# Hybrid block on one core: one ring of normalised rows, features read in place, and a wait ahead of GpSimd's additions

## The chip, the cores and the metric

The kernel runs on one core of one Trainium2 chip. The metric is the device time of one execution, in microseconds (us), as the median of several runs. The core has five engines with instruction streams of their own: TensorE (PE, with its weight loads shown as PEld), VectorE (DVE), ScalarE (ACT), GpSimd (POOL) and SyncE (SP), which here only issues transfers. They meet through semaphores. All share the on-chip memory SBUF; matmul results land in the eight banks of PSUM.

## What is computed

The input `x` is 4 sequences of 1024 rows of 256 numbers, f32, so 4096 rows. Four layers follow one another, each on the layer-normalised rows and added back to `x`:

```python
x = x + recurrent(_layernorm(x))   # LRU: a complex linear recurrence along time
x = x + sparse(_layernorm(x))      # same weights both times
x = x + attention(_layernorm(x))   # 8 heads of 64, keys and values through a rank-64 latent
x = x + sparse(_layernorm(x))
```

The recurrent layer, per chunk of time:

```python
u = einsum('btd,edh->ebth', x, W_in) + b_in          # three products: real, imaginary, o
h = scan(h = lam * h + gamma * (u[0] + i u[1]))       # lam = exp(-nu + i theta)
out = h.real @ W_mid[0] - h.imag @ W_mid[1] + o
y = gelu(out @ w1 + b1) @ w2 + b2 + out
y = layernorm(y) * ln_g + ln_b
```

The sparse layer, with two score branches ("out" and "in") that share one form:

```python
xc = einsum('ngf,gf->ng', x.reshape(n, 64, 4), conv_w) + conv_b
xa = gelu(batchnorm(xc))                               # statistics over all 4096 rows
score = softmax(xa @ lin_w.T + lin_b)                  # 256 scores of a row
out_branch = top32(score_out) * (x @ weight)           # the other 224 columns are zero
in_branch  = (top32(score_in) * x) @ weight
return out_branch + in_branch + bias
```

## The kernel before

`x` stays in SBUF from the first layer to the last, as 32 tiles of 128 rows. Each engine has its own block of code that runs the layers one after the other; all order is made by semaphores, and the order on each engine is written out by hand.

**Recurrent layer** (about 33 to 288 us of the span). It goes over 8 chunks of 512 rows with `over_chunks`, which calls each engine's `lru_step(n, c, behind, ahead1, ahead2, ahead4)`. The steps are pipelined: in step n VectorE makes `sums` (L1235, L1236), two `scan` pairs (L1244) and `turned_back` (L1252, L1253, L1258, L1261) of chunk n+1, the statistics and `centred` of chunk n-1, `turned_in` (L1227, products of PSUM and a table in SBUF) of chunk n+2, and layer-norm statistics of chunk n+4 (`ln_stats`, only while n+4 < 8) and of the finished chunk n-1 (`next_stats`). VectorE counts its ten main steps of a chunk on `l_dve`. TensorE in step n makes the o-product and the state product of chunk n (L1584, L1597), the input products of chunk n+2 (`lru_u`, L1556, in two halves), and the two products of the gated part (L1612, L1624 to L1630). GpSimd makes in step n, in this order: `turned_back` part 0 of chunk n+1 (L545), `rstd2(n-1)` (L557, L559), `turned_back` part 1 (L545), `residual(n-1)` (L565: x + y, 128x1024), `rstd(n+4)` (L532 to L538), `add_ln_bias(n+2)` (L550: x + ln_b, 128x1024) and `next_rstd(n-1)` (L577 to L585). Before step 0 it makes `add_ln_bias(0)`, `turned_back(0, 0)`, `rstd(2, 2)`, `turned_back(0, 1)`, `add_ln_bias(1)`.

**Sparse layers** (288 to 500 us and 1208 to 1418 us), `ffn(f)` on each engine, f = 0 and 1. ScalarE first applies the gelu to the features `xcT` (128 x 4096): the first two tiles of 128 columns into two small buffers `xa` (L972), then all eight chunks of 512 columns in place (L977), chunk 0 last because the small buffers are read from it. Then 32 tiles of 128 rows run in a software pipeline. For tile t ScalarE makes a normalised copy of the rows for the transposes (`ffn_z`, into `zf`, L878), the transposed copy (`ffn_zT`, L894), a copy of the tile's features (`ffn_xa`, L929), the logits' copy (`ffn_logits`, L900), the exponentials (`ffn_exp`, L913), exponentials with the winners masked (`ffn_rest`, L920), `ffn_sT`, `ffn_fs`, `ffn_gs` (L947, L942, L935), and a second copy of the same normalised rows for the gating (`ffn_zs`, into `zs`, L878 too, since both call `z_tile`). VectorE finds the 32 largest of 256 scores twice per tile: 8 MAX8 (L1380) and 8 MATCH_REPLACE8 (L1385), and one reciprocal (L1406). GpSimd's `tail` (L663 to L682) makes 7 elementwise operations; L667 multiplies the weights by `zs`. TensorE makes the transposes (L1694, L1720) and products (L1701, L1703, L1711, L1724). In the first sparse layer each engine also calls `head(t)`, which prepares the attention of sequence 0: ScalarE normalises 8 tiles (L1012) in tiles 8 to 15 and copies transposes (L1020), keys and queries in tiles 12 to 28.

**Attention** (500 to 1194 us) is not touched.

## Time and profile before

| | |
|---|---|
| median of 3 runs | 1422.08 us (1419.39 to 1425.52) |
| the profiled execution | 1419.8 us |
| its span, first to last instruction | 1418.1 us |
| PE busy | 1219.2 us (86%) |
| DVE busy | 1183.4 us (83%) |
| ACT busy | 1094.3 us (77%) |
| POOL busy | 992.4 us (70%) |

In the rows further down, a timeline line gives start and duration in us, engine, line, operation, what it writes and reads, and its count; neighbouring instructions of one line are merged into one row (x2, x4), and a bracket gives the engine's idle time before it and what ended that. A stretch (two times joined by a colon) gives its length and the busy time of each engine within it. Buffers carved out of the large scratch tile all show as `arena`, PSUM as `banks`.

The chain of work that ended last is PE 43%, DVE 22%, issue 17%, ACT 13%, POOL 4%. These shares are averages over layers with different limits, so the busy time of each engine is read stage by stage. The page's slices for the whole run (each digit is the busy share of one fortieth of the span, in tenths; PEclk is the granted TensorE clock):

```profile
PE   4999989757677679999999999999999999667776
DVE  7999999489999988777787778877878854799997
ACT  3332333688899679999999998999998994898886
PEclk9999999989999999999999999999999999799997
```

### The profile page before, as it was taken

What the parts mean: (1) busy time and instruction counts of PE and PEld (TensorE: products, weight loads), DVE (VectorE), ACT (ScalarE), POOL (GpSimd) and SP (SyncE); (2) the same over time, 40 slices, a digit from 0 to 9 for tenths busy, and PEclk for the clock granted to TensorE, in tenths of its full rate; (3) what the DMA queues carried; (4) which work ended last, traced back from release to release, by engine and by line L of the source; (5) the groups of instructions that cost most, each with busy time, mean ns of one, the idle gap of its engine ahead of it and who ended that gap; (6) DMA issues with size and microseconds to landing.
All of it is one profiled execution on the core that took longest, in us unless ns stands there. A gap on an engine that the chain in (4) does not pass through costs nothing.

```text
span 1418.1 us, 30913 instructions
## 1 busy us (share of the span) xinstructions
PE 1219.2 (86%) x10172; PEld 746.1 (53%) x10172; DVE 1183.4 (83%) x3173; ACT 1094.3 (77%) x2471; POOL 992.4 (70%) x1129
## 2 busy tenths in 40 slices
PE   4999989757677679999999999999999999667776
PEld 2455445434444335565666666666666667344443
DVE  7999999489999988777787778877878854799997
ACT  3332333688899679999999998999998994898886
POOL 4356753368788867767877677787777874398887
PEclk9999999989999999999999999999999999799997
DMA  6200000000000000000000000000000000000000
GB/s 169 74 1 1 0 0 1 1 1 1 1 1 1 1 1 2 2 3 2 2 2 2 2 2 2 2 2 2 2 2 2 2 2 1 1 31 16 31 16 31
DMA packets 27067, 14.84 MB, mean 10 GB/s; under 512 B 15062, under 2 KB 26652, under 8 KB 26908
## 3 DMA queue, kind: packets, MB, share of 16 engines
q1 hardware_dynamic: 26908, 12.87, 3.5%
q8 instruction: 82, 1.34, 0.4%
q14 instruction: 77, 0.63, 0.1%
HBM read 8.60 MB, written 4.19 MB: 9 GB/s over the span
## 4 chain that ended last, share of the span: by engine, by line
PE 43%; DVE 22%; issue 17%; ACT 13%; POOL 4%; DVEq 0%; DMA 0%; SPq 0%; POOLq 0%; ACTq 0%
PE banks L1848 6%; PE banks L1850 5%; DVE arena L1385 5%; PE banks L1837 5%; DVE arena L1380 4%; ACT arena L1056 4%; PE banks L1798 4%; PE banks L1774 3%; PE banks L1866 3%; PE banks L1865 3%; PE banks L1867 3%; ACT arena L1064 2%; DVE arena L1244 2%; DVE arena L1227 2%; POOL arena L726 2%
## 5 line engine op out<-in xcount | busy, mean ns | idle before, releaser
L726 POOL TENSOR_TENSOR arena<-arena 128x512 f16<-128x512 f32 x384 | 440.6, 1164 | 156.9 <-ACT arena L1064 152.1
L1056 ACT ACTIVATE arena<-banks 128x512 f32<-128x512 f32 x512 | 304.3, 600 | 53.8 <-PE banks L1850 49.9
L1459 DVE TENSOR_REDUCE arena<-banks 128x1 f32<-128x512 f32 x512 | 327.2, 679 | 9.5 <-PE banks L1837 6.4
L1064 ACT ACTIVATE arena<-arena 128x512 f16<-128x512 f32 x512 | 316.3, 633 | 0.0
L1865 PE MATMUL banks<-arena 128*128 128x65 f16 x2048 | 214.4, 193 | 6.1 <-POOL arena L726 5.8
L1866 PE MATMUL banks<-arena 128*128 128x64 f16 x2048 | 214.5, 195 | 0.0
L1867 PE MATMUL banks<-arena 128*128 128x65 f16 x2048 | 213.6, 192 | 0.0
L1483 DVE TENSOR_TENSOR arena<-arena 128x512 f16<-128x512 f32 x128 | 106.3, 830 | 125.0 <-ACT arena L1064 124.6
L1865 PEld LDWEIGHTS banks<-arena 128*128 128x128 f16 x2048 | 190.9, 96 | 35.3 <-issue 9.3
L1385 DVE MATCH_REPLACE8 arena<-arena 128x256 f32<-128x256 f32 x512 | 205.8, 409 | 1.1 <-issue 0.8
L1848 PE MATMUL banks<-arena 128*128 128x512 f16 x512 | 194.1, 379 | 14.2 <-ACT arena L1056 12.3
L1866 PEld LDWEIGHTS banks<-arena 128*128 128x128 f16 x2048 | 190.3, 97 | 28.3
L1380 DVE MAX8 arena<-arena 128x8 f32<-128x256 f32 x512 | 190.2, 413 | 13.6 <-ACT arena L900 9.3
L1837 PE MATMUL banks<-arena 128*128 128x512 f16 x512 | 194.3, 381 | 4.2 <-DVE arena L1459 4.2
L1850 PE MATMUL banks<-arena 128*128 128x512 f16 x512 | 193.7, 378 | 0.0
L1867 PEld LDWEIGHTS banks<-arena 128*128 128x128 f16 x2048 | 190.4, 99 | 0.0
L1724 PE MATMUL banks<-fW,arena 128*128 128x256 f32 x256 | 81.8, 447 | 42.8 <-ACT arena L947 42.8
L1837 PEld LDWEIGHTS banks<-arena 128*128 128x128 f16 x512 | 57.9, 113 | 71.5 <-DVE arena L1459 11.9
L1848 PEld LDWEIGHTS banks<-arena 128*128 128x128 f16 x512 | 50.4, 98 | 57.9 <-ACT arena L1056 35.8
L1724 PEld LDWEIGHTS banks<-fW,arena 128*128 128x128 f32 x256 | 47.5, 206 | 63.1 <-ACT arena L947 58.6
L1711 PE MATMUL banks<-fW,arena 128*128 128x256 f32 x256 | 78.7, 438 | 0.0
L781 ACT ACTIVATE zT<-banks 128x512 f32<-128x512 f32 x48 | 26.4, 601 | 64.6 <-PE banks L1543 64.6
(200 smaller groups left out, 2681.8 us busy)
## 6 DMA issues: line engine op xcount, KB each, us to landing
x<-in_L_attn_a_x SPq DMA_DIRECT2D x8, 512.0 KB, 3.9
out<-x SPq DMA_DIRECT2D x8, 512.0 KB, 2.9
arena<-arena SPq DMA_DIRECT2D x64, 1.0 KB, 1.9
arena<-in_L_attn_a_W_in SPq DMA_DIRECT2D x1, 768.0 KB, 5.7
arena<-in_L_attn_a_W_mid SPq DMA_DIRECT2D x1, 512.0 KB, 7.4
arena<-in_L_attn_a_w_w SPq DMA_DIRECT2D x2, 256.0 KB, 7.7
arena<-in_L_attn_b_Wq SPq DMA_DIRECT2D x1, 512.0 KB
arena<-in_L_attn_b_Wo SPq DMA_DIRECT2D x1, 512.0 KB
```

The source lines that it names most:

```text
L726: nc.gpsimd.tensor_tensor(pr_lo[c][:, kt, :], pr[:, kt, :], pr_hi[c][:, kt, :], ALU.subtract).then_inc(a_lP, 1)
L1056: nc.scalar.activation(pr[:, kt, :], ps[6 + kt % 2][:, :], ACT.Exp, scale=SM_SCALE).then_inc(a_P, 1)
L1064: nc.scalar.activation(pr_hi[c][:, kt, :], pr[:, kt, :], ACT.Copy).then_inc(a_hi, 1)
L1380: nc.vector.max(m8[p][:, i, r, :], src).then_inc(f_k[i], 1)
L1385: nc.vector.match_replace(wk[p][:, i, r % 2, :], m8[p][:, i, r, :], src, TAKEN).then_inc(f_k[i], 1)
L1459: nc.vector.tensor_reduce(mx_half[c][:, i // 2, i % 2:i % 2 + 1], ps[n % MAX_BANKS][:, :], X, ALU.max).then_inc(a_mx, 1)
L1837: mm(ps[n % MAX_BANKS][:, :], every[:, j, :], kA[B % 2][:, half * CH:half * CH + CH], start=True, stop=True).then_inc(a_mps, 1)
L1848: mm(o[:, :], kA[B % 2][:, kt * P:kt * P + P], qA[:, slot, c * CH:c * CH + CH], start=True, stop=False)
L1850: mm(o[:, :], kB[B % 2][:, kt * P:kt * P + P], qB[:, slot, c * CH:c * CH + CH], start=False, stop=True).then_inc(a_sps, 1)
L1865: mm(o, pr_hi[c][:, kt, js], lat[B % 2][:, kt, 0:1 + HD], start=kt == 0, stop=False)
L1866: mm(o[:, 1:1 + HD], pr_hi[c][:, kt, js], lat[B % 2][:, kt, 1 + HD:], start=False, stop=False)
L1867: last = mm(o, pr_lo[c][:, kt, js], lat[B % 2][:, kt, 0:1 + HD], start=False, stop=kt == KT - 1)
```

## The change

1. Sparse layers: `zs` and `ffn_zs` are gone. `zf` becomes a ring of four buffers (`Z_RING = 4`), written once per tile by `ffn_z`; both the transposes and GpSimd's product (L667) read it. `ffn_z` waits until the product of the tile four before has been made.
2. Sparse layers: `xa`, `ffn_xa` and the copies of features (L929) are gone; TensorE's logits read `xcT` in place. The gelu runs in place over tile 0, tile 1, the other half of chunk 0, then chunks 1 to 7.
3. Recurrent layer: a new GpSimd wait, `turned_whole(n)`, holds until all ten VectorE steps of chunk n are done. It stands ahead of `residual(n-1)` in each step that has a next chunk, and ahead of `add_ln_bias(0)`. `add_ln_bias(0)` moves behind both parts of `turned_back(0)` and `rstd(2, 2)`; `add_ln_bias(1)` moves into step 0.

```diff
--- before.py
+++ after.py
@@ -38,6 +38,7 @@
 GROUP = 4
 GROUPS = NH // 2
 Q_RING = 4
+Z_RING = 4
 
 
 B_IN, P_LOG, B_MID, W1B, W2B = 0, 6, 12, 16, 18
@@ -158,10 +159,8 @@
         after_rows = room[0]
 
 
-        zf = [carve([D]) for _ in range(2)]
-        zs = [carve([D]) for _ in range(2)]
+        zf = [carve([D]) for _ in range(Z_RING)]
         zfT = [carve([KB2, P]) for _ in range(2)]
-        xa = [carve([P]) for _ in range(2)]
         lg = [carve([2, D]) for _ in range(2)]
         wk = [carve([2, 2, D]) for _ in range(2)]
         m8 = [carve([2, ROUNDS, 8]) for _ in range(2)]
@@ -281,8 +280,7 @@
         f_bn = sem("f_bn_step")
         f_xa_all = sem("f_gelu")
         f_z = sem("f_z")
-        f_zs = sem("f_z_gating")
-        f_xa = sem("f_xa")
+        f_g01 = sem("f_gelu_first_tiles")
         f_tps = sem("f_zT_psum")
         f_zT = sem("f_zT")
         f_lps = sem("f_logits_psum")
@@ -544,6 +542,10 @@
                 pool.wait_ge(l_dve, n * L_STEPS + 4)
                 nc.gpsimd.tensor_tensor((pa, pb)[part], g[0], (cosT, sinT)[part], ALU.mult).then_inc(l_pool, 1)
 
+            def turned_whole(n):
+
+                pool.wait_ge(l_dve, n * L_STEPS + L_STEPS)
+
             def add_ln_bias(n):
                 pool.wait_ge(s_z, n + 1)
                 rows = x[:, bass.ds(n * TPC, TPC), :]
@@ -604,11 +606,11 @@
                     nc.gpsimd.affine_select(out=cvs[:, k, i, :], in_=cvb[:, i, k * P:k * P + P],
                                             compare_op=ALU.is_equal, fill=0.0, base=0,
                                             pattern=[[1, P]], channel_multiplier=-1).then_inc(s_prep, 1)
+            turned_back(0, 0)
+            turned_back(0, 1)
+            rstd(2, 2)
+            turned_whole(0)
             add_ln_bias(0)
-            turned_back(0, 0)
-            rstd(2, 2)
-            turned_back(0, 1)
-            add_ln_bias(1)
 
             def lru_step(n, c, behind, ahead1, ahead2, ahead4):
                 if ahead1:
@@ -617,9 +619,11 @@
                     rstd2(n - 1)
                 if ahead1:
                     turned_back(n + 1, 1)
+                    turned_whole(n + 1)
                 if behind:
                     residual(n - 1)
                 if n == 0:
+                    add_ln_bias(1)
                     rstd(3, 3)
                 if ahead4:
                     rstd(n + 4, n + 4)
@@ -663,8 +667,8 @@
                 nc.gpsimd.tensor_tensor(dd[p][:, 1, :], ex[p][:, 1, :], exr[p][:, 1, :],
                                         ALU.subtract).then_inc(f_d, 1)
                 pool.wait_ge(f_d, T * 2 + 1)
-                pool.wait_ge(f_zs, T + 1)
-                nc.gpsimd.tensor_tensor(sx[p], dd[p][:, 1, :], zs[p], ALU.mult).then_inc(f_s, 1)
+                pool.wait_ge(f_z, T + 1)
+                nc.gpsimd.tensor_tensor(sx[p], dd[p][:, 1, :], zf[t % Z_RING], ALU.mult).then_inc(f_s, 1)
                 pool.wait_ge(f_er, T * 2 + 2 + CREDIT["f_er"])
                 nc.gpsimd.tensor_tensor(dd[p][:, 0, :], ex[p][:, 0, :], exr[p][:, 0, :],
                                         ALU.subtract).then_inc(f_d, 1)
@@ -878,15 +882,10 @@
                 return nc.scalar.activation(dst.unsqueeze(1), x[:, bass.ds(t, 1), :], ACT.Identity,
                                             bias=rs[:, bass.ds(t, 1), 1], scale=rs[:, bass.ds(t, 1), 0])
 
-            def ffn_z(f, t, p):
-                z_tile(t, zf[p]).then_inc(f_z, 1)
-
-            def ffn_zs(f, t, p):
+            def ffn_z(f, t):
                 T = t + f * NT
-                if not (isinstance(T, int) and T < 2):
-                    act.wait_ge(f_s, T - 1)
-                    act.sem_inc(s_turn, 1)
-                z_tile(t, zs[p]).then_inc(f_zs, 1)
+                wait_from(act, f_s, T - Z_RING + 1)
+                z_tile(t, zf[t % Z_RING]).then_inc(f_z, 1)
 
             def ffn_zT(f, t, p):
                 T = t + f * NT
@@ -920,14 +919,6 @@
                     nc.scalar.activation(exr[p][:, i, :], wk[p][:, i, 1, :], ACT.Exp,
                                          bias=nm[p][:, i:i + 1]).then_inc(f_er, 1)
 
-            def ffn_xa(f, t, p):
-
-                T = t + f * NT
-                if not (isinstance(T, int) and T < 2):
-                    act.wait_ge(f_lps, T - 1)
-                    act.sem_inc(s_turn, 1)
-                nc.scalar.activation(xa[p], xcT[:, bass.ds(t * P, P)], ACT.Copy).then_inc(f_xa, 1)
-
             def ffn_gs(f, t, p):
 
                 T = t + f * NT
@@ -946,6 +937,10 @@
                 act.wait_ge(f_sps, T + 1)
                 nc.scalar.activation(sxT[p], ps[4][:, 0:D].rearrange("p (k c) -> p k c", k=KB2),
                                      ACT.Copy).then_inc(f_sT, 1)
+
+            def gelu(at, cols):
+                return nc.scalar.activation(xcT[:, at:at + cols], xcT[:, at:at + cols], ACT.Gelu,
+                                            bias=bn_bias[:, 0:1], scale=bn_scale[:, 0:1])
 
             def ffn(f):
                 base = LN_FFN2 if f else LN_FFN1
@@ -963,27 +958,21 @@
                         zT_chunk(n + (base + 1), 1 - c, 2 * (1 - c))
                     zT_chunk(base + NCH - 1, 1, 2)
                 for p in range(2):
-                    ffn_z(f, p, p)
-                    ffn_zs(f, p, p)
+                    ffn_z(f, p)
                     ffn_zT(f, p, p)
                 act.wait_ge(f_bn, 5 * (f + 1))
                 act.wait_ge(f_xc, NCH * (f + 1))
                 for t in range(2):
-                    nc.scalar.activation(xa[t], xcT[:, t * P:t * P + P], ACT.Gelu,
-                                         bias=bn_bias[:, 0:1], scale=bn_scale[:, 0:1]).then_inc(f_xa, 1)
-                for n in (1, 2, 3, 4, 5, 6, 7, 0):
-                    if n == 0:
-                        act.wait_ge(f_xa, NT * f + 2)
-                    nc.scalar.activation(xcT[:, n * CH:n * CH + CH], xcT[:, n * CH:n * CH + CH], ACT.Gelu,
-                                         bias=bn_bias[:, 0:1], scale=bn_scale[:, 0:1]).then_inc(f_xa_all, 1)
+                    gelu(t * P, P).then_inc(f_g01, 1)
+                gelu(2 * P, CH - 2 * P).then_inc(f_xa_all, 1)
+                for n in range(1, NCH):
+                    gelu(n * CH, CH).then_inc(f_xa_all, 1)
                     if n in (1, 3):
                         ffn_logits(f, n // 2, n // 2)
-                act.wait_ge(f_xa_all, NCH * (f + 1))
                 ffn_exp(f, 0, 0)
                 for t in range(NT - 2):
                     q = t % 2
-                    ffn_z(f, t + 2, q)
-                    ffn_xa(f, t + 2, q)
+                    ffn_z(f, t + 2)
                     ffn_rest(f, t, q)
                     ffn_zT(f, t + 2, q)
                     ffn_exp(f, t + 1, 1 - q)
@@ -992,7 +981,6 @@
                         head(t)
                     ffn_sT(f, t, q)
                     ffn_fs(f, t, q)
-                    ffn_zs(f, t + 2, q)
                     ffn_gs(f, t, q)
                 ffn_rest(f, NT - 2, 0)
                 ffn_exp(f, NT - 1, 1)
@@ -1690,8 +1678,9 @@
                 pe.wait_ge(f_z, T + 1)
                 if not (isinstance(T, int) and T == 0):
                     pe.wait_ge(f_zT, T + 0)
+                z = zf[t % Z_RING]
                 for k in range(KB2):
-                    last = nc.tensor.transpose(ps[0][:, k * P:k * P + P], zf[p][:, k * P:k * P + P], ident[:, :])
+                    last = nc.tensor.transpose(ps[0][:, k * P:k * P + P], z[:, k * P:k * P + P], ident[:, :])
                 last.then_inc(f_tps, 1)
 
             def ffn_logits(f, t, p):
@@ -1699,8 +1688,11 @@
                 if not (isinstance(T, int) and T == 0):
                     pe.wait_ge(f_lg, T + 0)
                 mm(ps[1][:, :], bias_ones[:, :], bias_rows[:, :], start=True, stop=False)
-                pe.wait_ge(f_xa, T + 1)
-                mm(ps[1][:, :], xa[p], lin[:, :], start=False, stop=True).then_inc(f_lps, 1)
+                if t < 2:
+                    pe.wait_ge(f_g01, 2 * f + t + 1)
+                else:
+                    pe.wait_ge(f_xa_all, NCH * f + t // TPC + 1)
+                mm(ps[1][:, :], xcT[:, t * P:t * P + P], lin[:, :], start=False, stop=True).then_inc(f_lps, 1)
 
             def ffn_full(f, t, p):
 
```

## Rows read from the trace of the kernel before

**Rows 1.** Stretches, busy us: PE, PEld, DVE, ACT, POOL; PEclk; DMA share; GB/s

```profile
111.50:137.30 25.80, 25.80 (x81) 13.63 (x80) 25.69 (x41) 8.55 (x16) 16.41 (x13) 1.00 0.00 1
...
163.30:196.40 33.10, 28.23 (x83) 14.26 (x82) 31.88 (x57) 8.66 (x16) 21.11 (x19) 0.95 0.00 1
```

**Rows 2.** Timeline, VectorE, recurrent layer: start, duration (us), line

```profile
47.49 6.07 DVE L1244 TENSOR_TENSOR_SCAN arena<-arena 128x512 f32<-128x512 f32 x2
...
99.95 3.02 DVE L1253 TENSOR_TENSOR arena<-arena 128x1024 f32<-128x1024 f32 x1
...
112.57 3.02 DVE L1236 TENSOR_TENSOR arena<-arena 128x1024 f32<-128x1024 f32 x1
...
126.27 2.67 DVE L1252 TENSOR_TENSOR arena<-arena 128x1024 f32<-128x1024 f32 x1
...
128.86 1.21 DVE L1253 TENSOR_TENSOR arena<-arena 128x1024 f32<-128x1024 f32 x1
...
175.74 6.04 DVE L1244 TENSOR_TENSOR_SCAN arena<-arena 128x512 f32<-128x512 f32 x2
```

**Rows 3.** Timeline of GpSimd, recurrent layer

```profile
46.01 1.01 POOL L535 TENSOR_TENSOR rs<-var_eps,minus_half 128x4 f32<-128x4 f32 x1
...
49.56 2.92 POOL L550 TENSOR_TENSOR x<-x,arena 128x1024 f32<-128x1024 f32 x1
...
111.51 3.00 POOL L550 TENSOR_TENSOR x<-x,arena 128x1024 f32<-128x1024 f32 x1
...
125.86 1.99 POOL L565 TENSOR_TENSOR x<-x,arena 128x1024 f32<-128x1024 f32 x1
...
177.79 2.91 POOL L565 TENSOR_TENSOR x<-x,arena 128x1024 f32<-128x1024 f32 x1
```

**Rows 4.** Two VectorE lines over the run: count, min/median/max ns

```profile
L1227 DVE SCALAR_TENSOR_TENSOR arena<-banks,arena x64: 718/737/752, 33.3 to 218.0; 128x512 f32<-128x512 f32 x64
...
L1244 DVE TENSOR_TENSOR_SCAN arena<-arena x32: 1192/1257/3320, 41.0 to 232.6; 128x512 f32<-128x512 f32 x32
```

**Rows 5.** Timeline, TensorE, recurrent layer; in brackets idle before, releaser

```profile
58.28 7.14 PE L1597 MATMUL banks<-arena 128*128 128x512 f32 x16 [1.73 <-DVE arena L1261]
...
85.59 1.09 PE L1543 MATMUL banks<-ident,zrow 128*128 128x128 f32 x8 [2.09 <-ACT zrow L774]
...
175.96 3.68 PE L1612 MATMUL banks<-arena 128*128 128x512 f32 x8 [1.28 <-DVE arena L1282]
...
183.23 5.37 PE L1556 MATMUL banks<-zT,arena 128*128 128x512 f32 x8 [3.59 <-DVE arena L1227]
```

**Rows 6.** VectorE's waits up to 290 us: total, times, longest

```profile
DVE xcT L1324 <- PE banks L1576: 12.4, 4, 5.2
```

**Rows 7.** Groups of instructions by line, whole run: busy us, mean ns

```profile
L878 ACT ACTIVATE arena<-x,rs 128x256 f32<-128x256 f32 x128 | 75.6, 594 | 0.0
...
L929 ACT ACTIVATE arena<-xcT 128x128 f32<-128x128 f32 x60 | 17.8, 296 | 0.0
```

**Rows 8.** Stretches as in rows 1, here of both sparse layers

```profile
384.04:402.76 18.72, 13.47 (x49) 8.52 (x49) 17.80 (x76) 17.11 (x50) 14.92 (x22) 0.91 0.00 1
...
402.76:420.94 18.18, 13.31 (x51) 8.00 (x52) 16.84 (x71) 16.60 (x50) 14.44 (x22) 1.00 0.01 1
...
422.00:440.00 18.00, 13.36 (x53) 7.86 (x53) 17.94 (x75) 16.43 (x49) 15.10 (x22) 1.00 0.00 1
...
1263.60:1304.70 41.10, 30.75 (x107) 18.57 (x107) 40.90 (x177) 36.33 (x108) 35.56 (x50) 0.92 0.08 27
```

**Rows 9.** Timeline of VectorE, first sparse layer: a wait for the attention's keys

```profile
416.13 0.69 DVE L1435 TENSOR_TENSOR arena<-banks,arena 64x512 f16<-64x512 f32 x1 [1.19 <-ACT arena L1026]
```

**Rows 10.** Timelines of VectorE and ScalarE, starts of both sparse layers

```profile
303.65 0.75 DVE L1380 MAX8 arena<-arena 128x8 f32<-128x256 f32 x2 [1.00 <-issue]
...
1230.55 0.75 DVE L1380 MAX8 arena<-arena 128x8 f32<-128x256 f32 x2 [0.88 <-issue]
...
1220.16 3.62 ACT L977 ACTIVATE xcT<-xcT,bn_bias,bn_scale 128x512 f32<-128x512 f32 x5
```

## The prediction

> **What bounds the kernel now.** I read the busy time of each engine stage by stage, then the timelines of the two engines that meet in each stage, then the waits of the one that is busiest. The stages must be taken apart, because the change touches two of them through different resources.
>
> In the recurrent layer two engines are full. In a middle stretch TensorE is busy 25.80 of 25.80 us and VectorE 25.69 of 25.80; later TensorE is busy only 28.23 of 33.10 us while VectorE has 31.88 [rows 1]. So TensorE's work sets the pace where VectorE keeps up, and VectorE's lateness shows as TensorE waits. There are four that VectorE causes: 1.73, 2.09 (by way of a normalised chunk on ScalarE, whose statistics VectorE made late), 1.28 and 3.59 us [rows 5]. After the last, eight matmuls take 5.37 us where eight of the same shape took 3.68 just before [rows 5]: the granted clock is 0.95 over that stretch, 1.00 in the other [rows 1].
>
> Why VectorE is late is in its own timeline. The same operation, two SBUF inputs of 128x1024, takes 1.21 us at best and 2.67 or 3.02 in other places [rows 2]. Each long one lies across a GpSimd add: the 2.67 of 126.27 ends 1.09 after the add that runs 125.86 to 127.85, and the 3.02 of 112.57 ends 1.08 after the add that ends at 114.51 [rows 2, 3]. So one engine runs and the other stands until it is finished. A pair of scans, 2.4 us when alone (two of 1.19), takes 6.07 and 6.04 beside adds [rows 2, 4]. By contrast L1227, one input from PSUM and one from SBUF, is 718 to 752 ns in all 64 cases [rows 4], with GpSimd adds beside several of them.
>
> In the sparse layers VectorE is full: 40.90 of 41.10 us, with ScalarE at 36.33 [rows 8]. Work taken from ScalarE is worth nothing there. It is worth something only where VectorE falls short: in the first sparse layer's middle tiles, where attention's preparation is added to ScalarE (VectorE 17.80 of 18.72 and 16.84 of 18.18, against 17.94 of 18.00 afterwards [rows 8]), and at both starts [rows 10].
>
> **The change part by part, recurrent layer.** `turned_whole` makes `residual` start after L1261 instead of beside L1252, L1253 or a scan. What is queued behind it on GpSimd: `residual(n-1)`, `rstd(n+4)`, `add_ln_bias(n+2)`, `next_rstd(n-1)`. The part products that VectorE itself waits for stand ahead of it. In its new place the add (1.99 us when unblocked [rows 3]) lies beside four L1227 (some 2.7 us), which never stretch [rows 4]. In steps 0 to 3 `rstd(n+4)` waits for statistics that VectorE makes only after these products, so it loses nothing, and `add_ln_bias(n+2)` behind it keeps its place, across `sums`: the 3.02 us of 112.57 stays [rows 2]. VectorE's `next_stats` wants the residual, and finds it ready with about 0.6 us to spare in steps 4 and 5 (2.7 less 1.99), more before. In step 6 there is no L1227, so VectorE will stand there for 2.1 us; it then has a 5.2 us wait for TensorE [rows 6], which covers this.
>
> VectorE's savings in order:
> - Setup: the scan pair of 6.07 us stood behind L545 and then behind `add_ln_bias(1)` (49.56, 2.92 with its own waiting) [rows 2, 3]. The second L545 now precedes `rstd(2)`, beside L1227; `rstd(2)` (a power of 1.01 us [rows 3] and three smaller operations, by my estimate 1.6 in all) takes its place beside the scans. Gain 6.07 - 2.4 = 3.7 if its small operations slip between, 2.1 if the scans wait for all of them. I take 2.9.
> - One L1253 from 3.02 to 1.21: 1.8. Two L1252 from 2.67 to 1.21 (the second a chunk later): 2.9. The pair of 6.04, which pays for the add of 177.79 (2.91, of which about 1.9 running): 1.7 [rows 2, 3]. Together 6.4.
> - Two more adds of this kind lie later, where TensorE already sets the pace: nothing.
>
> What of it reaches TensorE: at 58.28 its own earlier work allows only the wait of 1.73; at 85.59 the whole of the 2.9 arrives (1.73 + 2.09 = 3.8 would be the limit) [rows 5]. From there to 175.96 TensorE has no wait to lose; then 1.28 and 3.59 go, since VectorE is 4.7 and 6.4 us earlier by those points [rows 5]. With the wait of 3.59 the slow clock behind it goes too: 5.37 - 3.68 = 1.7 [rows 5]. Recurrent layer: 2.9 + 1.3 + 3.6 + 1.7 = 9.5 us; with the bounds of the first term 8.7 to 10.3.
>
> Two rules of the Trainium skill bear on this. SBUF — State Buffer, Who interferes with whom, says that a VectorE operation with two SBUF inputs and a GpSimd operation that reads SBUF shut each other out for a whole instruction, and that one with a single SBUF input does not take part. By that rule the residual beside L1227 costs nothing, and the trace agrees (718 to 752 ns [rows 4]); but the rule also says that every add left beside `sums` goes on costing its length, which speaks against a larger gain than mine. TensorE: Matmul & The Clock Gate, Loop structure matters more than you think, says that a long wait inside a loop of matmuls drops the clock. By it the 1.7 goes with the wait; if it stayed, the layer's sum would be 7.8.
>
> **Sparse layers.** Per tile ScalarE loses one L878 (594 ns) and one L929 (296 ns) [rows 7], 0.89 us of about 5.2 per tile (36.33 over seven tiles [rows 8]). GpSimd's and TensorE's instructions keep their number. The new ring wait asks for a product four tiles old, which ScalarE's own order (it copies the transpose of that product two tiles earlier) has already waited for: nothing. In 54 or so of the 64 tiles the saving only widens ScalarE's waits, since VectorE is the bound [rows 8].
> - Middle tiles of the first: VectorE's shortfall is 0.92 + 1.34 = 2.3 us [rows 8], 1.19 of it one wait for attention's keys behind ScalarE [rows 9]. It is all ScalarE's lateness, and 0.89 per tile over the seven tiles is 6: gain 2.1 (0.2 is the shortfall usual elsewhere).
> - Starts: the second `ffn_z` per tile goes before the batch statistics are ready, so it is hidden. The gelu of a whole chunk 0 becomes one of 256 columns ahead of the first logits: they come up to 0.3 us later in the first sparse layer; but four gelus of 0.72 (3.62 / 5 [rows 10]) instead of five lie ahead of the first exponential. Net on it -0.4 and -0.7. VectorE waits 1.00 and 0.88 us there for tile 2's logits [rows 10], which hang on that exponential: gain 0.4 and 0.8, bounds 0 and 1.9 together. I take 1.2.
>
> **Sum.** 9.5 + 2.1 + 1.2 = 12.8 us. The profiled execution took 1419.8 us (span 1418.1); it becomes 1407.0. It lies 2.3 below the median of 1422.08, so for a median I take 1422.1 - 12.8 = 1409.3.
>
> **The rivals.**
> - *Blocking comes back elsewhere.* VectorE arrives earlier and its scans meet GpSimd's small operations or the remaining adds more often; VectorE stays late at 183. For it: the pair of 6.04 still has L545 ahead of it. Against it: GpSimd's instructions hang on VectorE's own steps and so keep their relative place. Half of the recurrent gain: 4.8, total 8.1, 1414.0.
> - *The change doesn't do what it says in the recurrent layer.* TensorE's pace hides all, or the setup's new order delays `rstd(2)` as much as it frees. For it: TensorE is full in the middle stretch [rows 1]. Against it: its four waits [rows 5]. Only 2.1 + 1.2 = 3.3: 1418.8.
> - *The sparse layers give nothing.* ScalarE waits for TensorE inside the tile, not for its own work. 9.5 alone: 1412.6.
> - *Slower: L1227 is blocked as well.* Up to 183 us seven adds of 1.99 then stand across VectorE, 13.9 us, against 8.3 paid now (1.9 in the setup and the 6.4 above): +5.6 where VectorE sets the end, less 3.3 from the sparse layers: 1424.4. It decides once an add stretches the four L1227 beside it by more than 1.2 us (8.3 / 7). Against it: 64 durations without one stretched [rows 4].
>
> **How the numbers follow.** Forecast 0.60, blocking comes back 0.17, recurrent layer unchanged 0.09, sparse layers nothing 0.10, slower 0.04. The likeliest time is 1409.3, rounded 1409. The bounds of the terms give 8.7 + 1.5 + 0 = 10.2 to 10.3 + 2.3 + 1.9 = 14.5, so 1407.6 to 1412; three runs before lie 6 us apart, which adds about 3 either way. The range 1403.5 to 1416.5 takes in the first rival and the third, and leaves out the second and the fourth. About 0.5% (7.1 us, below 1415.0) is what a measurement can tell from no change: faster 0.83 (the forecast, the third rival, most of the first), same 0.14, slower 0.03.
>
> **What would show it.** After: L1252 and L1253 at 1.21 us everywhere; L1227 still under 0.76; `residual` right behind L1261; L1236 of 3.0 still there in the chunks that had it; no TensorE wait for VectorE between 100 and 230 us and no granted clock below 1.00 there; a wait of about 2 us before `next_stats` once, near 230. In the sparse layers: ScalarE's busy share down by a sixth, VectorE's shortfall in the middle tiles gone, the second half of all tiles as long as before. It is wrong if TensorE shows new waits for normalised chunks or if VectorE's tiles in the sparse layers change length.

## The result and the profile after

| | before | changed |
|---|---|---|
| median, beside each other | 1422.24 us (4 runs) | 1406.23 us (1404.81 to 1408.29, 4 runs) |
| ratio, 95% interval | | 0.9887 [0.9867, 0.9908] |
| profiled execution, its span | 1419.8, 1418.1 us | 1408.29, 1406.4 us |
| PE, DVE, ACT, POOL busy | 1219.2, 1183.4, 1094.3, 992.4 us | 1217.1, 1170.5, 1053.2, 990.1 us |

Faster by 1.1%, 1406.2 where 1409 was forecast. The two profiled executions differ by 11.5 us, the medians by 16.0; the experiments below show where part of that gap is from.

**Recurrent layer.** First the stretches that answer [rows 1] (columns as there), moved by the shift of the chunks (5.45 and 8.10 us):

```profile
106.05:131.85 25.80, 25.80 (x81) 13.65 (x80) 25.47 (x47) 8.66 (x16) 17.77 (x16) 1.00 0.00 1
155.20:188.30 33.10, 33.10 (x108) 17.73 (x107) 31.88 (x59) 9.63 (x18) 19.31 (x19) 1.00 0.00 1
```

The second held 28.23 us of TensorE at a clock of 0.95; now it is full, at 1.00. VectorE's timeline, against [rows 2]:

```profile
47.58 2.40 DVE L1232 TENSOR_TENSOR_SCAN arena<-arena 128x512 f32<-128x512 f32 x2
...
96.36 1.21 DVE L1241 TENSOR_TENSOR arena<-arena 128x1024 f32<-128x1024 f32 x1
...
107.18 3.02 DVE L1224 TENSOR_TENSOR arena<-arena 128x1024 f32<-128x1024 f32 x1
...
132.84 3.02 DVE L1224 TENSOR_TENSOR arena<-arena 128x1024 f32<-128x1024 f32 x1
...
167.60 4.35 DVE L1232 TENSOR_TENSOR_SCAN arena<-arena 128x512 f32<-128x512 f32 x2
```

and its line on PSUM (once L1227) over the run, as in [rows 4]:

```profile
L1215 DVE SCALAR_TENSOR_TENSOR arena<-banks,arena x64: 719/739/752, 33.4 to 207.1; 128x512 f32<-128x512 f32 x64
```

The setup's scan pair fell from 6.07 to 2.40, L1253 (now L1241) from 3.02 to 1.21, the later pair from 6.04 to 4.35. The two 3.02 of the second sum stayed, with GpSimd's bias beside them. GpSimd, against [rows 3]:

```profile
125.59 2.00 POOL L567 TENSOR_TENSOR x<-x,arena 128x1024 f32<-128x1024 f32 x1 [5.07 <-DVE arena L1249]
...
131.77 3.00 POOL L552 TENSOR_TENSOR x<-x,arena 128x1024 f32<-128x1024 f32 x1
...
229.75 2.00 POOL L567 TENSOR_TENSOR x<-x,arena 128x1024 f32<-128x1024 f32 x1 [5.83 <-DVE arena L1249]
```

The residual (L567) waits for VectorE's last step and takes 2.00 us; the four L1215 beside it keep their length. TensorE, against [rows 5]:

```profile
82.02 1.09 PE L1531 MATMUL banks<-ident,zrow 128*128 128x128 f32 x8 [1.25 <-ACT zrow L778]
...
170.76 3.60 PE L1600 MATMUL banks<-arena 128*128 128x512 f32 x8
174.19 3.60 PE L1544 MATMUL banks<-zT,arena 128*128 128x512 f32 x8
...
221.57 1.08 PE L1564 MATMUL banks<-zT,conv 128*64 128x512 f32 x4 [2.42 <-ACT zT L785]
250.50 1.55 PE L1531 MATMUL banks<-ident,arena 128*128 128x128 f32 x8 [1.82 <-ACT arena L778]
```

The waits of 1.73, 1.28 and 3.59 us are gone, that of 2.09 is 1.25, and the eight matmuls that took 5.37 take 3.60. So 85.59 has become 82.02 (3.57 earlier), and the matmuls that began at 232.37 with the same wait of 2.42 begin at 221.57: 10.80 earlier. Then 1.7 us go again: at 250.50 TensorE runs at half clock for a while (1.55 for eight transposes that took 1.07), which the profiled execution of the kernel before did not do here (261.31 with a full clock).

**Sparse layers.** The middle tiles, for [rows 8], the first two stretches shifted by 9.08 us and the third by 10.14. VectorE makes one reciprocal per tile (L1406, now L1394), and its start marks the tile:

```profile
374.96:393.68 18.72, 14.15 (x52) 8.98 (x52) 18.62 (x80) 14.60 (x43) 15.23 (x22) 0.91 0.01 1
393.68:411.86 18.18, 13.92 (x55) 8.39 (x54) 17.51 (x74) 14.65 (x42) 15.11 (x22) 1.00 0.00 1
411.86:429.86 18.00, 13.53 (x54) 8.00 (x53) 17.94 (x76) 14.64 (x42) 14.94 (x22) 1.00 0.00 1
```

VectorE's shortfall of 0.92 + 1.34 us has become 0.10 + 0.67; ScalarE is busy 14.60 instead of 17.11. In the third stretch VectorE had 17.94 and has 17.94.

**The ledger**, how much earlier the changed kernel's profiled execution is:

| at | us earlier |
|---|---|
| TensorE, 85.59 to 82.02 | 3.57 |
| TensorE, 232.37 to 221.57 | 10.80 |
| TensorE, 270.27 to 261.15 (half clock at 250) | 9.12 |
| batch statistics of the first sparse layer, 285.93 to 275.90 | 10.03 |
| its 14th reciprocal, 381.20 to 372.12 | 9.08 |
| its last, 490.99 to 480.06 | 10.93 |
| batch statistics of the second, 1211.94 to 1200.53 | 11.41 |
| its last reciprocal, 1407.31 to 1395.23 | 12.08 |
| span | 11.7 |

At the first sparse layer's start 0.95 us go again. The first tile's logits, two matmuls, ran at half clock there (2.08 us), in the kernel before at a full one (1.12).

### The profile page after: what moved, and what is told of

It reads as the page before. It is cut to its first block, busy times and chain, and to the rows that moved or that the text cites. A ratio compares the mean times of both kernels' runs of the same rounds, so it can differ in the third digit from the quotient of the medians.

```text
span 1406.4 us, 30669 instructions
## 1 busy us (share of the span) xinstructions
PE 1217.1 (87%) x10172; PEld 746.1 (53%) x10172; DVE 1170.5 (83%) x3173; ACT 1053.2 (75%) x2347; POOL 990.1 (70%) x1129
## 4 chain that ended last, share of the span: by engine, by line
PE 54%; issue 14%; ACT 13%; DVE 13%; POOL 5%; DVEq 0%; DMA 0%; SPq 0%; POOLq 0%; ACTq 0%
PE banks L1840 6%; PE banks L1842 6%; PE banks L1829 5%; DVE arena L1373 5%; PE banks L1585 4%; ACT arena L1044 4%; PE banks L1790 4%; DVE arena L1368 4%; PE banks L1544 3%; PE banks L1766 3%; PE banks L1858 3%; PE banks L1857 3%; PE banks L1859 3%; ACT arena L1052 2%; POOL arena L730 2%
## 5 line engine op out<-in xcount | busy, mean ns | idle before, releaser
L1840 PE MATMUL banks<-arena 128*128 128x512 f16 x512 | 194.6, 380 | 13.4 <-ACT arena L1044 11.4
L926 ACT ACTIVATE arena<-banks,arena 128x256 f32<-128x256 f32 x64 | 30.3, 473 | 63.0 <-PE banks L1716 63.0
```

The costliest lines, as they stand in the source:

```text
L1840: mm(o[:, :], kA[B % 2][:, kt * P:kt * P + P], qA[:, slot, c * CH:c * CH + CH], start=True, stop=False)
```

## The experiments

In the table of this section "layer end" is the time from the 14th reciprocal of the first sparse layer to its last. A gain in us with an interval is worked out from the ratio to the kernel before; it can differ by some 2 us from the difference of the two medians, and where it matters both stand. Two parts are only compared by the same measure.

**The recurrent part alone.** The kernel before with the diff's hunks on GpSimd's recurrent steps:

```diff
-            add_ln_bias(0)
             turned_back(0, 0)
-            rstd(2, 2)
             turned_back(0, 1)
-            add_ln_bias(1)
+            rstd(2, 2)
+            turned_whole(0)
+            add_ln_bias(0)
...
                     turned_back(n + 1, 1)
+                    turned_whole(n + 1)
...
                 if n == 0:
+                    add_ln_bias(1)
```

> The kernel before with the recurrent layer's part alone: the new order of GpSimd's opening steps and the wait for VectorE's last step in each chunk; the sparse layers as before. Theory A (VectorE's additions and scans took 3.02, 6.07 and 6.04 us because GpSimd's additions lay beside them, and TensorE waited for them): 10 to 11 us of the change's gain are here, so 1411 to 1412.5 us beside 1422.2, ratio 0.992 to 0.993, and the chunk of TensorE's stream that began at 232.37 us before begins at 221 to 222. Rival B (a part of that gain is given back by TensorE's clock at the end of the layer, whatever the sparse layers look like): 7.5 to 9 us, 1413 to 1415 us.

Measured 1409.92 us beside 1421.16, ratio 0.9937 [0.9921, 0.9954]: 9.0 us, within 6.5 to 11.2; the medians differ by 11.2. In its trace TensorE reaches 221.87 with the same wait of 2.42, and the batch statistics are aggregated at 275.31 (before 285.93): 10.6 us. The trace is as theory A has it. The times do not decide between A and B, and what B describes did happen in the first profiled execution of the changed kernel (10.80 us at 221.57, 9.12 at 261.15).

**The sparse part alone**, the rest of the diff:

> The changed kernel with the recurrent layer put back as it was: ring of four rows, features in place, new order of the gelu. Theory A (the sparse layers' first tiles were bound by ScalarE and later ones by VectorE, so 0.89 us of ScalarE's work per tile counts only at the start): 3 to 3.5 us, so 1418.7 to 1419.3 us, ratio 0.9975 to 0.998; the intervals of the first sparse layer's tiles in the middle 5.82 to 7.2 us, the rest as before. Rival (the sparse layers gave nothing of their own and the change's later gains come with the shift of the clock's phase): within 1 us of 1422.2. If both parts add up, this one's difference and that of the recurrent layer alone sum to the changed kernel's 16 us, or to 11.5 us if the single executions' difference is the truer one.

Measured 1418.99 us, ratio 0.9984 [0.9972, 0.9996]: 2.3 us, 0.6 to 4.0. That is less than theory A's 3 to 3.5 and more than the rival's 1, and the interval excludes neither. The two parts add up to the whole: 11.3 by the ratios, where the changed kernel beside the same runs of the kernel before gave 12.4, and 13.4 by the medians, where it gave 14.0. The better evidence is in the traces of the two kernels that share the recurrent part: the 14th reciprocal falls at 370.64 with the old sparse layers and 370.65 with the new, the last at 480.70 and 478.68. That is 2.0 us, all in the middle tiles, and none at the first layer's start. In the second layer the third tile's reciprocal comes 28.08 us behind the batch statistics with the old, 27.38 with the new: 0.7.

**The changed kernel again, twice.**

> The changed kernel itself once more, beside the same runs of the kernel before. The two profiled executions differ by 11.5 us and the medians by 16.0. Theory A (the profiled execution of the changed kernel was a slow one of its own kernel, the clock's phase at 250 us having taken 1.7 us and more): a median of 1405 to 1407 us again, and a second trace whose stream after 250 us shows less slow clock. Rival (the 11.5 us is the change's worth, the rest is scatter of the runs before): a median of 1409 to 1411 us.

> The changed kernel a third time, as the company of the other two: 1405.5 to 1407.5 us, ratio to the kernel before 0.989 to 0.9915, and its stretch from the 14th tile's reciprocal to the last of the first sparse layer 107.6 to 108.1 us again.

Measured 1407.21 (ratio 0.9913 [0.9900, 0.9926]) and 1405.27 (0.9885 [0.9868, 0.9902]): with the first, 16.0, 14.0 and 16.7 us by the medians, 16.1, 12.4 and 16.4 by the ratios. The profiled executions took 1405.8 and 1406.3, so 14.0 and 13.5 below the 1419.8 of before, which is itself 1.2 to 2.4 below its medians. The same instructions as at 250.50 above, in the second execution:

```profile
250.81 1.07 PE L1531 MATMUL banks<-ident,arena 128*128 128x128 f32 x8 [1.82 <-ACT arena L778]
251.72 0.60 PE L1612 MATMUL banks<-arena 128*128 128x256 f32 x2
```

Here the clock is full, and the next wait, at 259.78, lies 10.49 us ahead of 270.27. The third execution has slow matmuls at 221.47 already (1.60 for four that take 1.08) and reaches that wait at 261.02. The kernel with the sparse part alone, whose recurrent layer is that of before, has them in its profiled execution too:

```profile
233.76 1.98 PE L1558 MATMUL banks<-zT,conv 128*64 128x512 f32 x4 [2.42 <-ACT zT L779]
...
264.27 1.87 PE L1525 MATMUL banks<-ident,arena 128*128 128x128 f32 x8 [1.82 <-ACT arena L772]
```

So the 1.7 us belongs to the execution, not to the change: theory A.

**The bias ahead of the statistics**, on the changed kernel:

```diff
+                if ahead2:
+                    add_ln_bias(n + 2)
                 if ahead4:
                     rstd(n + 4, n + 4)
-                if ahead2:
-                    add_ln_bias(n + 2)
```

> The changed kernel with GpSimd's addition of the bias for the chunk after next put right behind the residual's, ahead of the small operations on the statistics: where VectorE's sum still took 3.02 us beside it, it should take 1.2. Theory A (in the changed kernel TensorE waits for VectorE nowhere between 82 and 221 us, so what is left of the blocking is hidden): within 2 us of the changed kernel, 1404.5 to 1408.5 us. Rival (the remaining blocking still sets the pace through ScalarE or the statistics): 4 to 5 us faster, about 1401.5 to 1402.5 us. A third way is that the later statistics hold up ScalarE's rows: over 2 us slower.

Measured 1406.4 us, ratio 0.9901 [0.9886, 0.9915], the same as the changed kernel's 1407.21. VectorE's timeline, and GpSimd's behind it:

```profile
108.26 1.22 DVE L1224 TENSOR_TENSOR arena<-arena 128x1024 f32<-128x1024 f32 x1
...
115.18 4.51 DVE L1232 TENSOR_TENSOR_SCAN arena<-arena 128x512 f32<-128x512 f32 x2
```

```profile
115.26 3.34 POOL L543 TENSOR_TENSOR arena<-arena 128x1024 f32<-128x1024 f32 x1
```

The 3.02 is gone, and the blocking is back one step later: GpSimd, now early, puts its multiplication (3.34 us) beside the scans, which take 4.51 instead of 2.45. No long sum is left, but what they gained the scans lost, so this run moves the blocking and does not show what it costs. That the rest of it is hidden, as theory A says, is argued from TensorE's full stretch (25.80 of 25.80 us), not shown by this run.

**GpSimd's two additions cut**, on the kernel before (both `rows[:, :, 0:4]` and so on):

> The kernel before with nothing moved, but GpSimd's two large additions per chunk (residual and bias) cut to 4 of their 256 columns: it leaves out nearly all of the residual of the recurrent layer and of the bias, so it shows what VectorE's steps cost when nothing large of GpSimd's lies beside them. Theory A (VectorE's 3.02, 6.07 and 6.04 us are due to those additions): sums and turns all at 1.2 us, scan pairs at 2.3 to 2.5 us except beside GpSimd's multiplications, and a gain of 10 to 12 us over before, 1409 to 1411 us, close to what the recurrent part alone gave (1409.9). Rival (what the change won came from the shorter wait of ScalarE and TensorE for the residual, not from the blocking): the long steps stay, or the gain is far from 10 us.

Measured 1414.78 us, ratio 0.9950 [0.9930, 0.9969]: 7.1 us, 4.4 to 9.9. No sum or turn of VectorE takes as long as 1.4 us any more, as theory A has it, and TensorE's waits of 1.28 and 3.59 are gone. But the gain is no larger than that of moving the additions: the intervals of the two overlap, and the matmuls that began at 232.37 begin at 225.11 here and at 221.57 in the changed kernel. Half of these 3.5 us are no matter of blocking: behind a wait of 2.08 us TensorE ran at half clock for a while (8.61 us for sixteen matmuls that take 7.05 in the changed kernel and before).

```profile
84.92 8.61 PE L1598 MATMUL banks<-arena 128*128 128x512 f32 x16
```

With that put aside it is 1.9 us behind the changed kernel, and the setup shows all of it (VectorE, then GpSimd):

```profile
47.53 4.31 DVE L1245 TENSOR_TENSOR_SCAN arena<-arena 128x512 f32<-128x512 f32 x2
```

```profile
47.30 2.35 POOL L545 TENSOR_TENSOR arena<-arena 128x1024 f32<-128x1024 f32 x1
```

With the additions nearly gone, GpSimd's multiplication stands beside the scans all the same: 4.31, not 2.40. The expected 10 to 12 us was too high for two reasons: I had counted the additions alone as blockers (1.9 us), and the clock took 1.7 in the profiled execution. How often it did in the others is not known.

**The setup's order alone.**

> The kernel before with the new order of GpSimd's opening steps alone (the first bias after VectorE's last step of chunk 0, the second in the first chunk's step); no wait in the later chunks. Theory A (the scan pair at 47.49 was 6.07 us long for the first bias, and the shift reaches the end): scan pair 2.4 us, 3.6 us faster, 1417 to 1418 us. Rival (the first bias late in the layer holds up the first residual, or the later blocking takes the gain back at another phase): 1419.5 to 1422 us, with the waits of TensorE at 176 and 183 us longer than 1.28 and 3.59.

Measured 1419.77 us, ratio 0.9989 [0.9977, 1.0001]: 1.2 us by the medians, 1.6 by the ratio, and no clear verdict; theory A's 3.6 us did not come. In its trace the scan pair is 2.40 and TensorE passes the second chunk's transposes (85.59 before) at 83.49, with no wait: 2.1 us, because in this execution eight matmuls of the setup took 5.06 at a reduced clock where 3.6 is usual, 1.5 us. Behind that, as before:

```profile
173.88 3.68 PE L1617 MATMUL banks<-arena 128*128 128x512 f32 x8 [1.29 <-DVE arena L1287]
181.14 5.37 PE L1561 MATMUL banks<-zT,arena 128*128 128x512 f32 x8 [3.58 <-DVE arena L1232]
```

The waits are as long as in [rows 5], the slow 5.37 with them; they belong to the other edit. The 2.1 stays to 230.28 (2.09) and to the batch statistics (2.12).

**The second copy of the rows put back**, on the changed kernel (`zs` and `ffn_zs` in their old places; 0.59 us of ScalarE per tile):

> The changed kernel with the second copy of the normalised rows for GpSimd's gating put back (0.59 us of ScalarE per tile; the 0.30 us copy of the features stays out). Theory A (only the tiles in the middle of the first sparse layer and the first ones of the second had ScalarE late): two thirds of what the sparse part gave, so 1.3 to 2.3 us slower than the changed kernel's 1407.2 in the same company, 1408.5 to 1409.5 us, the steady tiles at 5.82 us all the same. Rival (what counted was the order of the gelu and the logits' wait, not the work): the same as the changed kernel within 0.7 us.

**The copy of the features put back**, on the changed kernel (`ffn_xa` behind `ffn_z`, 0.30 us per tile):

> The changed kernel with ScalarE's copy of each tile's features put back, and with it its wait for the logits two tiles back (0.30 us per tile, tiles 2 to 31); the rows still made once. Theory A (the middle of the first sparse layer took 2 us longer because ScalarE had 0.89 us more per tile; 0.59 us more did not show, so it is a threshold of the sum): 0.30 us more is hidden, the stretch from the 14th tile's reciprocal to the last stays at 107.6 to 108.0 us, same time as the changed kernel within 1 us. Rival (the copy's wait and its place ahead of the second half's exponentials count): that stretch 109.5 to 110.1 us as in the kernels with the old sparse layers, 1.5 to 2 us slower than the changed kernel in the same company.

| | us, median | layer end | ScalarE's extra |
|---|---|---|---|
| changed, three executions | 1406.2, 1407.2, 1405.3 | 107.94, 108.03, 107.71 | |
| second copy of the rows | 1406.0 | 107.70 | 0.59 |
| copy of the features | 1409.4 | 109.81 | 0.30 |
| recurrent part alone (both) | 1409.9 | 110.06 | 0.89 |
| before (both) | 1422.1 | 109.79 | 0.89 |

Ratios to before are 0.9891 [0.9874, 0.9908] for the rows' copy and 0.9912 [0.9893, 0.9932] for the features'. The larger copy costs nothing, the smaller one the whole 2 us; both times the rival's stretch came out and theory A's did not, and so it is not a threshold of ScalarE's sum. By the medians the smaller copy costs more than the stretch shows: 4.1 us beside the changed kernel's 1405.3 of the same set of runs. The traces don't show where the other 2 us are. Nor is it the copy's wait, which ended nothing: no idle time stands before L929. ScalarE's timelines show why. First the kernel with the rows' copy (L884 at 390.74), from one tile's gate (L935) to the next:

```profile
386.01 0.47 ACT L935 ACTIVATE arena<-banks,arena 128x256 f32<-128x256 f32 x1 [0.37 <-PE banks L1727]
...
390.74 0.61 ACT L884 ACTIVATE arena<-x,rs 128x256 f32<-128x256 f32 x1
391.72 0.47 ACT L935 ACTIVATE arena<-banks,arena 128x256 f32<-128x256 f32 x1 [0.37 <-PE banks L1727]
```

Then the one with the features' copy (L929):

```profile
395.66 0.47 ACT L935 ACTIVATE arena<-banks,arena 128x256 f32<-128x256 f32 x1 [0.86 <-PE banks L1727]
...
396.52 0.30 ACT L929 ACTIVATE arena<-xcT 128x128 f32<-128x128 f32 x1
...
401.57 0.47 ACT L935 ACTIVATE arena<-banks,arena 128x256 f32<-128x256 f32 x1 [0.86 <-PE banks L1727]
```

The rows' copy lies in ScalarE's wait for TensorE, which shrinks from 0.86 to 0.37: a turn of ScalarE's loop takes 5.71 us (391.72 - 386.01), as in the changed kernel (381.31 to 387.02 in its second execution). The features' copy lies ahead of that wait, in the loop: 5.91 (401.57 - 395.66), as with both copies (5.91). VectorE's tile takes 5.82. So with an attention item in the tile (0.58 us, in both turns above) the loop is 0.11 shorter or 0.09 longer than VectorE's tile. Two turns with the features' copy are longer still, 6.11 and 6.21; over the five turns from 377.44 to 408.42 ScalarE takes 30.98 us, where the changed kernel takes 29.68 (375.60 to 405.28): 1.3 of the 1.8 us between their layer ends. Without such an item a turn can take 5.44, and VectorE sets the pace either way.

**Idle matmuls at the start of the sparse layers**, on the changed kernel:

```diff
+                for _ in range((4, 1)[t] if t < 2 else 0):
+                    mm(ps[1][:, :], ident[:, :], lin[:, :], start=True, stop=True)
                 mm(ps[1][:, :], bias_ones[:, :], bias_rows[:, :], start=True, stop=False)
...
-                pe.wait_ge(f_z, T + 1)
                 if not (isinstance(T, int) and T == 0):
                     pe.wait_ge(f_zT, T + 0)
+                for _ in range(5 if t == 2 else 0):
+                    mm(ps[0][:, :], ident[:, :], lin[:, :], start=True, stop=True)
+                pe.wait_ge(f_z, T + 1)
```

> The changed kernel with ten matmuls that nobody reads, put on TensorE where it waits at the start of each sparse layer (four and one ahead of the first two tiles' logits, in waits of 2.79 and 0.94 us, five ahead of the third tile's transposes, in a wait of 4.79 us). Theory A (TensorE is granted half its clock after these waits, and the first tiles take 6.28 and 6.66 us instead of 5.82 for it): the matmuls after the waits at full clock, the first tiles 5.8 to 6.0 us, and 2 to 3 us faster than the changed kernel, 1404 to 1405 us. Rival (these tiles wait for ScalarE and VectorE whatever the clock): the same within 0.7 us, or slower where the added matmuls run over the end of a wait.

Measured 1403.53 us, ratio 0.9874 [0.9854, 0.9893]; 1.7 to 3.7 us below the changed kernel's three medians. The stretch from 280 to 290 us without them (changed kernel, second execution), columns as in [rows 1], and TensorE's timeline behind it:

```profile
280.00:290.00 10.00, 5.03 (x11) 2.86 (x12) 9.51 (x41) 8.97 (x19) 3.04 (x4) 0.50 0.00 1
```

```profile
288.99 0.69 PE L1683 MATMUL banks<-ident,arena 128*128 128x128 f32 x2 [4.79 <-ACT arena L882]
289.47 0.63 PE L1690 MATMUL banks<-bias_rows,bias_ones 65*128 65x512 bf16 x1
289.90 1.91 PE L1695 MATMUL banks<-lin,xcT 128*128 128x512 f32 x2
```

and the same two views with them:

```profile
280.00:290.00 10.00, 8.66 (x24) 4.01 (x24) 9.76 (x41) 9.05 (x19) 2.87 (x5) 1.00 0.00 1
```

```profile
282.83 4.45 PE L1681 MATMUL banks<-lin,ident 128*128 128x512 f32 x10
288.62 0.44 PE L1685 MATMUL banks<-ident,arena 128*128 128x128 f32 x2 [1.34 <-ACT arena L882]
...
289.11 1.02 PE L1699 MATMUL banks<-lin,xcT 128*128 128x512 f32 x2
```

The granted clock is 1.00 instead of 0.50 (2.4 instead of 1.2 GHz), the tile's logits take 1.02 instead of 1.91, and the first intervals between reciprocals are 5.81 and 5.81 instead of 6.28 and 6.35. From the batch statistics to the fifth reciprocal it is 37.49 us instead of 38.30 (39.28 and 39.30 in the other two executions) in the first layer, and 37.39 instead of 39.23 in the second. Theory A holds. The Trainium skill, TensorE: Matmul & The Clock Gate, Loop structure matters more than you think, has a loop in which a long DMA wait between matmuls drops the clock. Here the waits are for ScalarE, and the rows agree that the clock falls behind them; they also show that filling the waits keeps it.

**Three more at the end of each layer**, ahead of the last two tiles' transposes:

> The kernel with ten idle matmuls at the start of each sparse layer, and three more at its end, ahead of the last two tiles' transposes, where TensorE waits 2.80 and 1.36 us for GpSimd and the last layer's matmuls then run at half clock (1.87 and 1.91 us for four instead of 1.13 and 1.03). Theory A (the clock lost in these waits costs the layer's end): 0.5 to 1.5 us faster than the ten alone, 3.5 to 5 us faster than the changed kernel of the same company. Rival (the end hangs on GpSimd and VectorE, not on TensorE): as the ten alone, 2.5 to 3.7 us faster than the changed kernel.

Measured 1402.89 us, ratio 0.9873 [0.9853, 0.9894], 2.4 below the changed kernel in the same set of runs (1405.27). From the second layer's batch statistics to its last reciprocal it is 192.77 us, with the ten alone 192.71, and from there to the end of the span 10.6 against 10.0. So the last three brought nothing, and the number is the rival's. Its reason is not shown, though, since the three did not keep the clock where it was wanted. The last tile's matmuls and ScalarE's step behind them, with the ten alone:

```profile
1393.56 1.13 PE L1720 MATMUL banks<-fW,arena 128*128 128x256 f32 x4 [0.47 <-ACT arena L938]
```

```profile
1394.73 0.47 ACT L926 ACTIVATE arena<-banks,arena 128x256 f32<-128x256 f32 x1 [0.86 <-PE banks L1720]
```

and with the three:

```profile
1392.55 2.07 PE L1722 MATMUL banks<-fW,arena 128*128 128x256 f32 x4 [0.47 <-ACT arena L938]
```

```profile
1394.66 0.47 ACT L926 ACTIVATE arena<-banks,arena 128x256 f32<-128x256 f32 x1 [1.80 <-PE banks L1722]
```

With the ten alone the last tile ran at full clock anyway; the 1.87 and 1.91 us of half clock were the tile before it, and there the three helped (1.13 and 1.03) without bringing the last reciprocal forward. With the three the last tile itself ran at half clock, and ScalarE waits 1.80 us instead of 0.86: the last tile does hang on TensorE, by 0.9 us. These two kernels, the ten alone and the thirteen, have the lowest medians of all that ran, and the 0.6 us between them is within their scatter.

## Why the prediction was right, and where its steps were off

- **Setup**: the term was mis-sized, 2.9 for 3.57. The pair fell to 2.40, so the small operations of `rstd(2)` did slip between the scans (themselves stretched, 0.98 and 1.04 us for 0.19); the upper bound was the truth.
- **Blocking in the chunks**: right in place and size. L1252 and L1253 at 1.21 (one of 1.65 at 94.79 is left), L1236's 3.02 still there, L1227 (now L1215) untouched, 4.35 left of the second pair (6.04 - 1.7 = 4.3).
- **What reaches TensorE**: 10.80 at 221.57 against 9.5. All of it is there by the end of the two waits: the matmuls right behind the slow ones (L1624 at 188.43, L1612 at 177.63 after) are 10.80 earlier already, and the later chunks add nothing, as forecast. 3.57 came in the setup, 0.2 by 156 us, and 1.8 with the slow clock. The other two steps, between the starts of the same matmuls, gave 1.4 and 3.8 where the waits are shown as 1.28 and 3.59. So the setup's term is half of what was missing. The recurrent part alone measured 9.0 by the ratio, 11.2 by the medians.
- **The wait before `next_stats`**: 2.1 us forecast once, near 230; `231.90` on VectorE waited 2.22 for the residual of 229.75, and nothing came of it.
- **Middle tiles**: 2.1 forecast, 2.0 measured between the twin kernels (1.85 in the ledger). The size was right for a wrong reason. I divided by ScalarE's busy time ("0.89 per tile over the seven tiles is 6"); only the 0.30 us copy counted, and in its place in the loop, not in the sum.
- **Starts**: 0.4 and 0.8 forecast, about 0 and 0.7 measured. At the first start the clock swings by more than the term, and the sum had no term for that: from the batch statistics to the third reciprocal it is 27.4 us where the first tile's logits run at half clock (2.07 or 2.08 us), 25.8 to 26.5 where they run at a full one (1.12 to 1.20), with the new layers and with the old. Of the kernels with both edits of the sparse layers four executions of five had the half clock, of those with the old layers one of four; whether that is chance is not known.
- **Sum**: 12.8 forecast. Single executions give 11.5, 14.0 and 13.5, the medians 14.0 to 16.7, the ratios 12.4 to 16.4. The 1406.2 lies below the 1407.6 that the bounds of the terms allow and inside the range by what the scatter of the runs added. Missing were 0.7 from the setup and 0.6 behind it. The base, 1422.08 from three runs, lay 0.2 to 1.1 us above the later sets of 11 to 18 runs (1421.0 to 1421.9), which puts the forecast time that much too high. The rest of the gap is open. For the profiled execution 1407.0 was forecast, and the three took 1408.3, 1405.8 and 1406.3.
- **The rivals**: the blocking came back elsewhere where the bias was moved forward and where the additions were cut, not in the changed kernel. The one on the other side, L1227 blocked as well, had no basis: 719 to 752 ns in all 64.

Not settled: why the clock falls in one execution at 221, in another at 250 and in a third at neither, and whether the 2 us and more between the changes of the medians and of the traces is more than that.

## What to carry to other kernels

When two engines shut each other out for whole instructions, put the one that nobody waits for beside an instruction that does not take part, rather than make it shorter: moving GpSimd's additions gave no less than nearly deleting them, since without them one of its multiplications stands in the same place in the setup. Work taken from an engine counts only where it stands in that engine's loop, ahead of its wait; here a copy inside the wait was free, whatever the busy share says. And where TensorE waits some microseconds ahead of work that others wait for, a few matmuls that nobody reads can be worth as much as a whole edit: 1.7 to 3.7 us here, where the sparse layers' edit gave 2.3.

## What the runs showed of the hardware

- Scans on SBUF take part in the blocking: a pair takes 2.33 to 2.45 us alone, 4.31 to 4.51 beside one GpSimd multiplication of 128x1024, 6.07 beside a multiplication and an addition.
- GpSimd's operations of four columns stretch too: 0.19 us alone, 0.98 and 1.04 for those that start at 47.87 and 48.93, beside the scans.
- Same program, same inputs: the half clock after a TensorE wait of about 2 us comes in one place in one execution and elsewhere in the next (behind 2.42 us at 221.47, behind 1.82 us at 250.50), worth 1.6 to 1.7 us each time.
- Ten matmuls that nobody reads, put into waits of 2.79, 0.94 and 4.79 us, kept the granted clock at 1.00 where it was 0.50.
